# Four places of order in a layered attention kernel: the context's fourth sum, attention zero's first normalization, early input tiles, and a second tile ahead of the gates

## What is computed

```
x = x + L0_xattn(layernorm(x), ctx)
x = x + L0_ffn(layernorm(x))      # ternary weights, sigmoid gate, int8 activations
x = x + L1_xattn(layernorm(x), ctx)
x = x + L1_ffn(layernorm(x))      # ternary weights, silu gate, Hadamard transform of h
x = x + L2_xattn(layernorm(x), ctx)
x = x + L2_ffn(layernorm(x))
x = x + L3_xattn(layernorm(x), ctx)
x = x + L3_ffn(layernorm(x))      # weights from splines
```

## Time and profile before

| | us |
|---|---|
| median of 3 runs (lowest, highest) | 2167.9 (2162.09, 2168.79) |
| the profiled execution | 2166.01 |
| its span | 2164.2 |
| TensorE busy in it | 2036.5 (94%) |
| VectorE, ScalarE, GpSimd busy | 1152.8, 825.2, 182.0 |
| chain that ended last, on TensorE | 82% |
| mean granted clock of TensorE | 0.979 of full speed |

### The profile page before, as it was taken

The page is one execution under the profiler, slowest core; times in us unless marked ns, Lnnn a source line. Parts: engine busy times, 40 slices in busy tenths (PEclk is TensorE's granted clock), DMA queues, the critical chain, the costliest instruction groups (busy, mean ns, idle before and its releaser), DMA issues.

```text
span 2164.2 us, 28614 instructions
## 1 busy us (share of the span) xinstructions
PE 2036.5 (94%) x10533; PEld 1156.7 (53%) x10556; DVE 1152.8 (53%) x2597; ACT 825.2 (38%) x1717; POOL 182.0 (8%) x466
## 2 busy tenths in 40 slices
PE   8999999999999798999999999999689888888999
PEld 3444444444666344555555555466444455556665
DVE  1324455258122485675666666578556568864221
ACT  1333223312111264554544554455332245553331
POOL 1011110000000121110111111011000000000000
PEclk9999999999999999999999999999899989998999
DMA  5355342551641421020000001220000322210000
GB/s 232 134 214 202 154 160 92 211 200 53 211 148 64 150 104 47 22 101 22 24 26 23 22 22 44 92 78 21 19 16 13 134 92 85 91 55 6 11 11 15
DMA packets 60315, 185.12 MB, mean 86 GB/s; under 512 B 10578, under 2 KB 29010, under 8 KB 54463
## 3 DMA queue, kind: packets, MB, share of 16 engines
q1 hardware_dynamic: 58451, 145.55, 19.5%
q0 software_dynamic: 1728, 37.75, 4.5%
HBM read 124.61 MB, written 49.50 MB: 80 GB/s over the span
## 4 chain that ended last, share of the span: by engine, by line
PE 82%; DVE 12%; ACT 3%; issue 2%; DMA 1%; SPq 1%; POOL 0%; DVEq 0%; ACTq 0%
PE psum L120 58%; PE psum L113 8%; PE psum L1567 5%; PE psum L2594 5%; PE psum L1611 5%; DVE small L2473 2%; PE psum L1155 1%; PE psum L2402 1%; DVE R L1322 1%; DVE R L1321 1%; DVE WK L2479 1%; DMA R<-in_wkv 1%; DVE small L301 1%; DVE WK L324 1%; DVE WK L1312 0%
## 5 line engine op out<-in xcount | busy, mean ns | idle before, releaser
L120 PE MATMUL psum<-R,WK 128*125 128x512 f32 (+11 forms) x3080 | 1047.0, 486 | 30.9 <-DMA WK<-in_ctxT 7.5
L120 PEld LDWEIGHTS psum<-R,WK 128*112 128x112 f32 (+4 forms) x3094 | 504.1, 171 | 521.2 <-issue 407.8
L113 PE MATMUL psum<-small,WK 112*125 112x112 f32 (+5 forms) x2036 | 280.1, 268 | 65.9 <-DVE WK L1312 20.0
L113 PEld LDWEIGHTS psum<-small,WK 112*125 112x125 f32 (+5 forms) x2036 | 225.6, 155 | 171.7 <-issue 83.7
L120 PE MATMUL psum<-WK,R 128*32 128x128 f32 (+3 forms) x1752 | 201.3, 358 | 4.3 <-ACT WK L2433 1.9
L120 PE MATMUL psum<-R 128*128 128x112 f32 (+4 forms) x832 | 146.8, 326 | 10.5 <-DVE R L1928 9.3
L120 PEld LDWEIGHTS psum<-WK,R 128*32 128x32 f32 (+3 forms) x1752 | 109.7, 137 | 68.4 <-issue 20.7
L120 PEld LDWEIGHTS psum<-R 128*128 128x128 f32 (+2 forms) x832 | 102.8, 182 | 56.5 <-issue 41.4
L1661 ACT ACTIVATE WK<-psum,small 112x487 f32<-112x487 f32 x128 | 96.9, 757 | 76.7 <-DVE small L1746 72.7
L1567 PE MATMUL psum<-R,WK 128*112 128x512 f32 x256 | 120.1, 592 | 0.0
L1743 DVE TENSOR_TENSOR psum<-psum,R 112x112 f32<-112x112 f32 x128 | 35.1, 274 | 152.8 <-PE psum L120 152.8
(11 more groups left out here) (238 smaller groups left out, 2155.8 us busy)
## 6 DMA issues: line engine op xcount, KB each, us to landing
R<-in_wf POOLq DMA_DIRECT2D x6, 4096.0 KB, 13.7
d_w<-R POOLq DMA_DIRECT2D x6, 2048.0 KB, 19.5
R<-d_w SPq DMA_DIRECT2D x6, 2048.0 KB, 10.5
WK<-in_ctxT SPq DMA_DIRECT2D x16, 750.0 KB, 6.6
d_v<-WK SPq DMA_DIRECT2D x16, 750.0 KB
R<-in_wq SPq DMA_DIRECT2D x7, 1024.0 KB, 8.3
R<-in_wo SPq DMA_DIRECT2D x6, 1024.0 KB, 15.8
d_k<-X SPq DMA_DIRECT2D x8, 750.0 KB, 5.2
```

The lines of the kernel that those rows point to most:

```text
L113: ins = pe.transpose(dst, src, idn[0:k, 0:k])
L120: ins = pe.matmul(dst, lhs, rhs, start=k == 0, stop=k == len(pairs) - 1)
```

## The change

It alters the order of instructions at four places.

1. In blocks 0 to 5 of the context ScalarE's fourth sum stands behind the drain of `T_2`, no longer behind that of `k3_3`.
2. Statistics and normalization of attention zero's batch 0 become `first`, which VectorE runs in the context stage ahead of its wait for the last `kv_0`.
3. SyncE asks for tiles 0 and 1 of feed-forward one ahead of the coefficient stores of batches 6 and 7, for the others where it did before. The transposed activations of attention zero move from column 8192 to 9216 of R1, so that the two tiles have room.
4. In feed-forward two VectorE quantizes tile 1 and takes the statistics of tile 2 ahead of tile 0's gated products, and the sign copies stand behind that; TensorE waits for the signs one iteration later.

```diff
--- before.py
+++ after.py
@@ -574,7 +574,8 @@
                                 act.wait_ge(sem("k3_stored"), 16 * b)
                             ins = act.activation(k3o[:, j, :], src[:, 0:S], ACT.Identity, bias=bk3[:, j:j + 1])
                         ins.then_inc(act_ring.sem_drained, 1)
-                        if kind == "k3" and b < 6:
+                        j = dict(k3_0=0, k3_1=1, k3_2=2).get(name, 3 if name == f"T_{NS - 1}" else None)
+                        if j is not None and b < 6:
                             if j == 0:
                                 act.wait_ge(sem("context_raw"), 16 * (b + 1))
                                 if b:
@@ -582,6 +583,7 @@
                             act.activation(tern[:, j * 2048:(j + 1) * 2048], raw[:, j * 2048:(j + 1) * 2048], ACT.Abs,
                                            accum_out=wsum[:, b, j:j + 1]).then_inc(sem("context_abs"), 1)
                         if kind == "v2":
+                            j = int(name[-1])
                             act.wait_ge(sem("context_low"), NS * b + j + 1)
                             if NS * b + j:
                                 k = NS * b + j - 1
@@ -631,6 +633,8 @@
                                 coefficients(dve, link, 2)
                             if s == 2:
                                 split_coefficients(dve, link)
+                    if b == NB - 1:
+                        stages[0]["first"](dve)
                     dve_ring.wait_filled(dve, b, "kv_0")
                     if b:
                         dve.wait_ge(sem("kv2_stored"), 16 * b)
@@ -814,7 +818,7 @@
             W = Area(R1)
             wq, wk, wv, wo = (W.get(KT * D, kt=KT, e=D) for _ in range(4))
             xn = Area(R1, 11648).get(D, rows=T)
-            A = Area(R1, 8192)
+            A = Area(R1, 9216)
             xnT = A.get(KT * T, kt=KT, t=T)
             qT, kT = A.get(KT * T, kt=KT, t=T), A.get(KT * T, kt=KT, t=T)
             A = Area(WK)
@@ -852,7 +856,7 @@
                     sp.dma_start(d_cd[:, k], coefT[0:84, k % 8].rearrange("p s q -> p (s q)")
                                  ).then_inc(sem(f"coef_stored{k % 8}"), 16)
 
-            def sync(sp, load_next):
+            def sync(sp, load_next, load_tiles):
                 context_stored(sp)
                 load_ctxV(sp, 0)
                 load_ctxV(sp, 1)
@@ -870,6 +874,7 @@
                     dve_ring.wait_filled(sp, b - 2, "o")
                     load_ctxV(sp, b)
                     store_coefficients(sp, b - 2)
+                load_tiles(sp, range(2))
                 for b in (NB - 2, NB - 1):
                     store_coefficients(sp, b)
 
@@ -989,8 +994,6 @@
 
             def dve(dve):
                 link = dve_chain.on(dve)
-                dve.wait_ge(sem("x_loaded"), 16 * 5)
-                ln_stats(dve, link, n, 0)
                 for b0, b1, b2 in iterations(3):
                     if b2 is not None:
                         dve_ring.wait_filled(dve, b2, "pT")
@@ -1004,9 +1007,8 @@
                         dve_ring.wait_filled(dve, b2, "o")
                         dve.tensor_scalar(o, dve_ring.bank["o"][0:T, :], inv, None, ALU.mult
                                           ).then_inc(dve_ring.sem_drained, 1)
-                    if b0 is not None:
-                        if b0:
-                            act_ring.wait_filled(dve, b0 - 1, "xnT")
+                    if b0:
+                        act_ring.wait_filled(dve, b0 - 1, "xnT")
                         ln_apply(dve, n, b0, xn).then_inc(sem(f"{stage}_xn"), 1)
                     if b1 is not None:
                         dve_ring.wait_filled(dve, b1, "v")
@@ -1029,12 +1031,17 @@
                     if b2 == 2:
                         stages[2]["prepare"](dve)
 
+            def first(dve):
+                dve.wait_ge(sem("x_loaded"), 16 * 5)
+                ln_stats(dve, dve_chain.on(dve), n, 0)
+                ln_apply(dve, n, 0, xn).then_inc(sem(f"{stage}_xn"), 1)
+
             def pool(pool):
                 link = pool_chain.on(pool)
                 for b in range(NB):
                     ln_power(pool, link, n, b)
 
-            return dict(load=load_weights, load_ctxT=load_ctxT, sync=sync, pe=pe, act=act, dve=dve, pool=pool)
+            return dict(load=load_weights, load_ctxT=load_ctxT, first=first, sync=sync, pe=pe, act=act, dve=dve, pool=pool)
 
 
         def ternary_ffn(stage, n, m0, qb, silu, hadamard, last_values=None):
@@ -1085,11 +1092,11 @@
                 if hadamard and 0 in mats:
                     sp.dma_start(had, io.hadamard).then_inc(sem(f"{stage}_weights"), 16)
 
-            def sync(sp):
+            def sync(sp, tiles=range(NT)):
 
                 if hadamard:
                     last_values(sp)
-                for i in range(NT):
+                for i in tiles:
                     if i >= 2:
                         sp.wait_ge(sem(f"{stage}_x{i % 2}"), arrived[i - 2])
                     for b, of, to in pieces(i):
@@ -1161,6 +1168,7 @@
                         if i == 1:
                             x_ready(pe, n)
                             pe.wait_ge(sem(f"{stage}_weights"), 16 * 3)
+                        if i == 2:
                             pe.wait_ge(sem(f"{stage}_signs"), 1)
                         for c in range(FC):
                             if b2 is not None:
@@ -1282,11 +1290,6 @@
             def dve(dve):
                 x_ready(dve, n)
                 link = dve_chain.on(dve)
-                if hadamard:
-                    dve.wait_ge(sem(f"{stage}_weights"), 16 * 3)
-                    dve.tensor_copy(plus_minus[:, 0, :], had)
-                    dve.tensor_scalar(plus_minus[:, 1, :], had, -1.0, None, ALU.mult).then_inc(sem(f"{stage}_signs"), 1)
-
                 def gated(b, c):
                     k = FC * b + c
                     piece = h[:, c * 512:(c + 1) * 512]
@@ -1322,7 +1325,18 @@
                     link(dve.tensor_tensor(o[:, :, 1, :], a[:, :, 0, :], a[:, :, 1, :], ALU.subtract))
 
                 if hadamard:
+                    def next_x(b):
+                        quantize_x(dve, b)
+                        if b + 1 < NT:
+                            stats(dve, b + 1)
+
                     for b0, b1, b2, b3 in iterations(4, NT):
+                        if b1 == 0:
+                            next_x(b0)
+                            dve.wait_ge(sem(f"{stage}_weights"), 16 * 3)
+                            dve.tensor_copy(plus_minus[:, 0, :], had)
+                            dve.tensor_scalar(plus_minus[:, 1, :], had, -1.0, None, ALU.mult
+                                              ).then_inc(sem(f"{stage}_signs"), 1)
                         for c in range(FC):
                             if b1 is not None:
                                 if b2 is not None:
@@ -1330,10 +1344,8 @@
                                 gated(b1, c)
                         if b3 is not None:
                             quantize_h(b3)
-                        if b0:
-                            quantize_x(dve, b0)
-                            if b0 + 1 < NT:
-                                stats(dve, b0 + 1)
+                        if b0 and b1:
+                            next_x(b0)
                         if b2 is not None:
                             if b2:
                                 dve.wait_ge(sem(f"{stage}_hi"), b2)
@@ -2713,9 +2725,9 @@
         @block.sync
         def _(sp):
             context["sync"](sp)
-            stages[0]["sync"](sp, lambda sp, m: stages[1]["load"](sp, [m]))
+            stages[0]["sync"](sp, lambda sp, m: stages[1]["load"](sp, [m]), stages[1]["sync"])
             prologue_stored(sp)
-            stages[2]["load"](sp, stages[1]["sync"])
+            stages[2]["load"](sp, lambda sp: stages[1]["sync"](sp, range(2, NT)))
             stages[1]["back"](sp)
             if upto > 2:
                 stages[2]["sync"](sp, lambda sp: stages[3]["load"](sp, [0, 1]))
```

## The result

| | before | changed |
|---|---|---|
| median (lowest, highest; runs) | 2168.35 us (2162.09, 2168.85; 4) | 2141.36 us (2138.32, 2142.61; 4) |
| ratio, 95% interval | | 0.988 (0.9859 to 0.9901) |
| profiled execution, its span | 2166.01, 2164.2 | 2140.85, 2139.1 |
| mean granted clock | 0.979 | 0.983 |

The changed kernel is faster by 27.0 us in the medians and 25.2 in the profiled executions; 25.4 was forecast against the latter. In eight more runs of it, beside other kernels, its medians were 2143.06 and 2141.96; over all twelve runs the median is 2141.8 (2137.7 to 2147.0).

A forecast was written before the change was run, and what follows sets the result against it. TensorE, busy for 94% of the span, was taken to bound the kernel. Savings of 11.1 + 0 + 8.9 + 5.4 = 25.4 us from the profiled 2166.0 us gave 2140.6 us; range with the first two rivals 2134 to 2150.

The forecast's parts named there:

- Both kinds of wait: Context: TensorE's waits for turned-key drains (4 x 1.82 us) and turned-weight copies (2 x 1.9 us) go; 11.1 us.
- The cover for the later sum: Context: the sum ending about 1 us later is covered by VectorE's copies and 8.3 us of load slack; costs nothing.
- The wall: Attention zero: VectorE's copy of v waits 14.26 us for kv's store, so of 2.45 us about 0.8 arrive.
- the two cases I had laid out: Attention zero: 0.8 us gained by the waits alone, or 0.9 us lost with the clock; 0 taken between them.
- 6.5 + 2.4 = 8.9: Feed-forward one: gates start 6.5 us earlier without the late first tile, and the clock gives another 2.4 us.
- The clock's 2.4: Feed-forward one: first 31 gate products took 9.28 us against 6.85 in feed-forward two; 2.4 us saved without the wait.
- 0.4 + 3.4 + 1.6 = 5.4: Feed-forward two: 0.4 us of sign wait, 3.4 us of second-tile wait and 1.6 us of clock saved.
- that the clock stays low in parts 3 and 4: Both feed-forward stages: waits go without clock gains, and attention zero costs 0.9 us; 2145.5 us, chance 0.15.
- The soft wall: Attention zero: 2.5 us and up to 3.4 us of clock come through; 2134.7 us, chance 0.07.
- The early tiles: Feed-forward one: rival had SyncE reach its new tile requests late, making that part worth nothing; 2149.5 us, chance 0.03.
- a gain swallowed later: Later stages: one bounded by a transfer or VectorE leaves less than 6.5 us of gain; near 2163 us, chance 0.02.
- The slower rival: Context: later sum delays threshold, ternary weights and next raw load until ScalarE's first sum waits; 2173 us, chance 0.01.

The follow-up runs named there:

- the split: Changed kernel with the stores of the last block's two v results (125 rows) each cut into 112 and 13 rows: 2135.59 us, ratio 0.985.
- the split with earlier transposes: Changed kernel with cut v stores, plus TensorE starting attention zero's transposes before waiting for VectorE's last kv copies: 2134.31 us, ratio 0.9844.
- the one without part 2: Changed kernel with cut v stores, but attention zero's first normalization back behind the last kv copies: 2139.61 us, ratio 0.9868.

## Why the prediction was right, and where it was not

The time was right (2140.6 forecast, 2141.36 measured, 2140.85 in the profiled execution), in the main by its own terms. That it agrees to a few tenths is luck: the changed kernel's other two profiled executions took 2144.42 and 2137.74 us, and the local gains of the table add up to 11.21 + 0.73 + 9.18 + 5.47 = 26.6 us, less 0.65 at the start and 0.82 behind the last of the four places.

- **Part 1**, 11.1 forecast, 11.21 in the table, 11.7 later in the kernel that undoes it, 13 in its median. Both kinds of wait went whole. The cover for the later sum was costed at nothing, rightly: VectorE's total comes 2.74 us behind the kv product's start, 2.60 before, and with all four sums moved another 5.3 us were covered.
- **Part 2**, 0 forecast, 0.73 in the table (2.48 - 1.20 - 0.55), 0 in the median. The wall was read rightly from one row of VectorE, and the split shows it. At the exponentials' transposes, for which I had 0.8, the table has 2.48 - 1.20 = 1.28: 0.9 since the maximum no longer waits for TensorE, and 0.35 since the store landed that much sooner behind the kv product. The clock came out between the two cases I had laid out. Behind the shorter gap it stayed up in part: the 72 products after the first transposes took 12.43 us where they had taken 13.76. The wall swallows that, and TensorE's wait becomes 4.34 us, where I had 3.5 without this and near 7 with the clock wholly up. Behind the wait the clock costs 0.55 us more than before (and 1.7 us more than with part 2 undone: 5.44 against 3.74 us for 32 products), where I had 1.7. So 0 was a fair middle of the terms and not a derived value; that the medians show 0 as well is luck within their spread.
- **Part 3**, 6.5 + 2.4 = 8.9 forecast; 6.49 + 0.64 + 2.05 = 9.18 in the table, 9.0 when undone. My 6.5 was reckoned to the start of the gates, so 6.49 + 0.64 = 7.13 stands against it: I had the gates 1.7 us behind the start of the transposes (0.4 + 1.33, as in the earlier trace rows), and they came 1.15 behind, since the wait for the residual's addition (1.19 us in the earlier trace rows) went too and left 0.77 for ScalarE. The clock's 2.4 measured 2.05. The two errors nearly cancel.
- **Part 4**, 0.4 + 3.4 + 1.6 = 5.4 forecast; 0.43 + 3.35 + 0.01 + 1.68 = 5.47 in the table. As a sum of local terms it is right to 0.1 us. As a gain in the total it is not shown: undone, it costs nothing that can be measured. The step that failed there is the silent one, that whatever TensorE gains at a place is there at the end. I had put the chance of a later stage swallowing a gain at 0.02, and looked for it in transfers and VectorE; in the profiles it was the clock of stages that the change does not touch.
- **The sum**. The parts undone one at a time are worth 13, 0, 8 and 0 us, 21 together, and the change is worth 25 to 27. One program's runs spread over 3 to 12 us, so these medians are blunt, and only the local terms are sharp. Why the parts make less than the whole is not shown.

The rivals: that the clock stays low in parts 3 and 4 is out (1.00 in both windows). The soft wall is out, and hard wall and lost worth are shown by the split. The early tiles are early (asked for at 682.58). Of a gain swallowed later, this pair of profiles has only the 0.82 us. The slower rival's mechanism needs a delay that even all four sums moved back don't make.

## What to carry to other kernels

Price a removed wait from its row, then look at the clock behind the gap: where it was down (parts 3 and 4), it was worth another quarter to a half of the wait; behind the 1.82 us of part 1 it was up (1.00 in the earlier trace rows), and there was nothing to add. When a step is moved ahead of a wait, look for the next wait that does not depend on the engine you relieve, such as a store whose buffer is written over; take that one away first, and the reorder that measured zero may be worth something (2.1 us at its place here). Judge small parts by the starts of the same instructions in two profiles as well as by medians, and follow them to the end of the program, since later stages can give back at the clock what was gained.

## What was not expected of the hardware

- Cutting two stores of 125 rows each into 112 and 13 rows took the landing of the store behind them from 18.4 to 7.6 us after its issue.
- Gaps of 1.81 and 1.82 us ahead of the exponentials' transposes were followed by full clock in the split with earlier transposes (32 products in 3.74 us) and in the one without part 2 (3.74), and by half clock in the split alone (5.25); 1.64 us at the stage's start were followed by half clock in the changed kernel. In this range the gap's length alone does not tell.
- Extra products that nobody reads, put into an idle time, made the kernel some 3 us faster (ratio 0.9985, 0.9976 to 0.9995).
- Two programs that differ by 3.8 us at 1380 us had the same median; in their profiles the difference is made up by half clock 500 us later (0.87 against 0.91 over 80 us).
